# Attention layer for eight batches: in the last batch's steps 3 to 10 the second pair of scores goes ahead of the maxima, the turns of y and h use the job bank, and POOL makes h's output for batch 6

## The reference

```python
xn = layer_norm(x, norm_w, norm_b)
q = (xn @ q_w + q_b).reshape(Bx, Tx, H, -1)
k = (xn @ k_w + k_b).reshape(Bx, Tx, H, -1)
att = jnp.einsum('bnhl,bmhl->bnmh', q, k)
att = att + (1.0 - mask) * -1000000.0
att = jax.nn.softmax(att, axis=2)
v = ((xn @ v_w + v_b) * src_mask[:, :, None]).reshape(Bx, Tx, H, -1)
y = jnp.einsum('bnmh,bmhl->bnhl', att, v).reshape(Bx, Tx, Dx)
e = jax.nn.silu(emb) @ emb_w + emb_b
scale, shift = jnp.split(e[:, None, :], 2, axis=2)
h = layer_norm(y, sb_norm_w, sb_norm_b) * (1.0 + scale) + shift
h = jax.nn.silu(h) @ out_w + out_b
return x + h
```

## Time and profile before

| | |
|---|---|
| median of 3 runs | 521.43 us (519.89 to 522.01) |
| profiled execution | 522.72 us, its span 521.0 us |
| busy in the span | PE 503.0, DVE 408.0, ACT 356.2, POOL 225.3 us |
| clock of PE | full in all but the first slices |
| steps 3 to 10 of batch 7 | 465.42 to 494.47 us of the span |
| steps 11 to 15 of batch 7 | 494.47 to 506.8 us |
| last output products, norms and stores | 506.8 to 521.0 us |

### The profile page before, as it was taken

The page is one execution under the profiler, slowest core; times in us unless marked ns, Lnnn a source line. Parts: engine busy times, 40 slices in busy tenths (PEclk is TensorE's granted clock), DMA queues, the critical chain, the costliest instruction groups (busy, mean ns, idle before and its releaser), DMA issues.

```text
span 521.0 us, 10061 instructions
## 1 busy us (share of the span) xinstructions
PE 503.0 (97%) x2831; PEld 189.4 (36%) x2834; DVE 408.0 (78%) x657; ACT 356.2 (68%) x647; POOL 225.3 (43%) x270
## 2 busy tenths in 40 slices
PE   8898999999999999999999999999999999998787
PEld 3422333343333333333333434343433333332225
DVE  6696778888798978888788878888788877888714
ACT  2305777667876778677877777677777777666783
POOL 4365324436335643536335543545345444334101
PEclk9989999999999999999999999999999999999999
DMA  5335444234434443235434444235433342234002
GB/s 155 111 116 163 124 124 134 79 93 125 129 89 123 132 140 113 79 101 153 127 99 122 108 132 125 79 107 151 134 102 115 104 133 83 82 113 128 0 2 81
DMA packets 54586, 57.42 MB, mean 110 GB/s; under 512 B 12424, under 2 KB 41736, under 8 KB 54560
## 3 DMA queue, kind: packets, MB, share of 16 engines
q1 hardware_dynamic: 51808, 54.74, 36.0%
q10 hardware_dynamic: 2752, 2.37, 1.6%
HBM read 35.82 MB, written 21.00 MB: 109 GB/s over the span
## 4 chain that ended last, share of the span: by engine, by line
PE 85%; DVE 4%; issue 3%; POOL 3%; ACT 3%; DMA 1%; SPq 0%; POOLq 0%; ACTq 0%; DVEq 0%
PE pv_ps L577 24%; PE st_ps L561 22%; PE mx_ps L525 12%; PE job_ps L640 9%; PE job_ps L649 5%; PE job_ps L661 3%; DVE negmax L952 2%; PE mx_ps L686 2%; ACT probs L745 2%; PE mx_ps L538 2%; PE mx_ps L620 1%; PE mx_ps L694 1%; PE pv_ps L461 1%; DMA k_rows<-qk_dram 1%; DVE x_stats L956 0%
## 5 line engine op out<-in xcount | busy, mean ns | idle before, releaser
L952 DVE TENSOR_REDUCE negmax<-mx_ps 128x2 f32<-128x1024 f32 x256 | 304.7, 1219 | 83.2 <-PE mx_ps L525 82.9
L745 ACT ACTIVATE probs<-st_ps 128x512 f32<-128x512 f32 x502 | 272.3, 595 | 116.5 <-PE st_ps L561 115.8
L561 PE MATMUL st_ps<-q_rows,k_rows 115*128 115x512 bf16 x502 | 155.1, 383 | 3.2 <-ACT probs L745 2.8
L577 PE MATMUL pv_ps<-probs,v_rows 128*32 128x512 f32 x1024 | 136.4, 605 | 0.6 <-ACT probs L745 0.6
L1225 POOL TENSOR_TENSOR qk_parts<-qk_rest,qk_parts 128x512 bf16<-128x512 f32 x31 | 36.0, 1161 | 133.0 <-DVE qk_parts L1026 133.0
L525 PE MATMUL mx_ps<-k_rows,q_rows 51*128 51x512 bf16 x512 | 79.4, 383 | 2.1 <-DMA k_rows<-qk_dram 2.1
L561 PEld LDWEIGHTS st_ps<-q_rows,k_rows 115*128 115x128 bf16 x502 | 39.1, 97 | 105.0 <-ACT probs L745 71.7
L1210 POOL TENSOR_TENSOR qk_parts<-qk_full,zero 128x512 bf16<-128x512 f32 x29 | 30.2, 1042 | 77.1 <-ACT qk_full L767 77.1
L640 PE MATMUL job_ps<-x_norm_t,w_qk 128*128 128x512 f32 x116 | 59.5, 593 | 0.0
L525 PEld LDWEIGHTS mx_ps<-k_rows,q_rows 51*128 51x128 bf16 x512 | 15.8, 94 | 111.0 <-DVE negmax L952 53.0
L1216 POOL TENSOR_TENSOR qk_rest<-qk_full,qk_parts 128x512 f32<-128x512 f32 x31 | 35.9, 1158 | 4.3 <-ACT qk_parts L759 2.0
(11 more groups left out here) (126 smaller groups left out, 390.3 us busy)
## 6 DMA issues: line engine op xcount, KB each, us to landing
qk_dram<-qk_parts SPq DMA_DIRECT2D x128, 128.0 KB
q_rows<-qk_dram SPq DMA_DIRECT2D x124, 96.0 KB, 2.6
k_rows<-qk_dram SPq DMA_DIRECT2D x124, 96.0 KB, 2.6
x_in<-in_x SPq DMA_DIRECT2D x16, 256.0 KB, 3.0
x_res<-in_x SPq DMA_DIRECT2D x7, 512.0 KB, 4.4
out<-out_sb SPq DMA_DIRECT2D x14, 256.0 KB, 2.6
k_rows<-mask_dram SPq DMA_DIRECT2D x64, 6.0 KB
w_e<-in_L_cond_emb_w ACTq DMA_DIRECT2D x4, 256.0 KB, 2.9
```

Source lines behind the costliest of these rows:

```text
L561: pe.matmul(st_bank(b, t, h), k_rows[0:ROWS_ALL, g, h, c * P:(c + 1) * P], q_rows[0:ROWS_ALL, g, h, :], start=True, stop=True).then_inc(st ...
L577: mm = pe.matmul(pv_ps[VW * h:VW * (h + 1), :], v_rows[:, c, g * GH + h, :], probs[:, t % P_SLOTS, h, :], start=(c == 0), stop=(c == CH - ...
L745: act.activation(probs[:, t % P_SLOTS, h, :], st_bank(b, t, h), ACT.Exp).then_inc(exp_done, 1)
L952: dve.tensor_reduce(by_pair[:, :, j, c], mx_ps[j][:, :, :], AXIS_X, ALU.max, negate=True).then_inc(max_done, 1)
```

## The change

All of it concerns batch 7. `short(b, t)` holds for its steps from 3 on.

- PE's order in short steps: scores 0 and 1, value product, scores 2 and 3, small turn, quad, side. (In wide steps there are no quads left, and the order stays.)
- In short steps the sides use `job_ps` in place of the first bank of `mx_ps[0]`. They wait for `out_ready` of batch 5 and for the reader of the side before, and no longer for a reduction; the quad no longer waits for the reader of a side. ACT and DVE read the turned tile from there.
- The first of the late output products waits for the read of the third turn of y of batch 7, as both use `job_ps`.
- `h_t` of batch 6 is made by POOL with four `tensor_tensor` (two for each half), in place of two `scalar_tensor_tensor` on DVE. They stand in POOL's program behind the bias on x_res. `h_lin` enters twice: h_tanh * h_lin + h_lin.

```diff
-LAST_LATE = {(2, 1): ("proj", 3, 0), (7, 2): ("hturn", 0, -1), (8, 2): ("hturn", 1, -1)}
+LAST_LATE = {(2, 1): ("proj", 3, 0)}
+SHORT_STEP = 3
+def short(b, t):
+
+    return isinstance(b, int) and b == B - 1 and t >= SHORT_STEP
...
+        def side_bank(b, t):
+
+            return job_ps[:, :] if short(b, t) else mx_ps[0][:, 0, :]
...
-                    if j == 0 and side_at(b, t - 1):
+                    if j == 0 and side_at(b, t - 1) and not short(b, t - 1):
...
                 if i == 0 and 0 in halves:
                     pe.wait_ge(h_ready, KD * (B - 1))
-                    pe.wait_ge(out_ready, 2 * (B - 2))
+                    pe.wait_ge(y_ready, NG * (B - 1) + NG - 1)
...
-                ps = mx_ps[0][:, 0, :]
+                ps = side_bank(b, t)
...
+                if short(b, t):
+                    pe.wait_ge(out_ready, 2 * (B - 2))
...
-                pe.wait_ge(max_done, PAIRS * (STEPS * mb + step) + 1)
+                if not short(b, t):
+                    pe.wait_ge(max_done, PAIRS * (STEPS * mb + step) + 1)
...
-                    max_turn(b, t)
+                    if not short(b, t):
+                        max_turn(b, t)
...
                     pv_step(b, t)
-                    max_quad(b, t)
+                    if not short(b, t):
+                        max_quad(b, t)
                     if not wide(b, t):
                         st_unit(b, t, 2)
                         st_unit(b, t, 3)
+                    if short(b, t):
+                        max_turn(b, t)
+                        max_quad(b, t)
...
-                    act.activation(h_lin[:, i, :], mx_ps[0][:, 0, :], ACT.Identity, bias=mod_now[:, 1, i:i + 1],
+                    act.activation(h_lin[:, i, :], side_bank(b, t), ACT.Identity, bias=mod_now[:, 1, i:i + 1],
...
-                    by_head = mx_ps[0][:, 0, :].rearrange("p (c h w) -> p c h w", h=GH, w=VW)
+                    by_head = side_bank(b if t >= 0 else b - 1, t if t >= 0 else t + STEPS).rearrange("p (c h w) -> p c h w", h=GH, w=VW)
...
+                if isinstance(b, int) and b == B - 1:
+                    for i in range(KD):
+                        pool.wait_ge(h_tanh_ready, KD * (B - 2) + i + 1)
+                        pool.wait_ge(turned["outp"], 2 * (B - 2))
+                        pool.tensor_tensor(h_tanh[:, i, :], h_tanh[:, i, :], h_lin[:, i, :], ALU.mult).then_inc(h_mixed, 1)
+                        pool.wait_ge(h_mixed, i + 1)
+                        pool.tensor_tensor(h_t[:, i, :], h_tanh[:, i, :], h_lin[:, i, :], ALU.add).then_inc(h_ready, 1)
```

More of the change, by code:

```diff
@@ L352, in attention_layer @@
         h_tanh_ready = sem("h_tanh_ready")
+        h_mixed = sem("h_mixed")
         h_ready = sem("h_ready")
```

## The result

The changed kernel takes 518.37 us (median of 14 runs, 517.24 to 520.40) against 521.23 (14 runs, 519.87 to 522.03). The ratio is 0.9949 with a 95% interval of 0.9936 to 0.9962, so 2.7 us faster with an interval of 2.0 to 3.3. The prediction was 518.9. The gain lies at the edge between "faster by over 0.5%" and "within 0.5%", where the forecast had put it.

The account below looks back on a forecast made before the run. No engine was full; DVE was taken to bound steps 3 to 5 of batch 7, PE's written order the rest. Step 12 starting 2.5 us earlier, other terms 0, gave 518.9 us from the median 521.43; range 517.3 to 521.2.

Parts of the forecast that it names:

- The spacings: Times between operations on PE, ACT and DVE, read from the old trace; old order reproduced to about 0.15 us.
- the walk: Steps 3 to 12 of batch 7 worked through in the new order: step 12 starts 2.55 us earlier, say 2.5.
- One sign of being right: Step 12's first score waits on the rows' DMA and starts 2.2 to 2.3 us after the last split.
- The side turns: Turns of h in steps 6 and 7 and of y in step 9: 1.63, 2.03 and 2.72 us earlier.
- rival 3: Side turns still wait for a reduction while quads go later: 2.1 us slower, 523.5; chance 0.05.
- The rows of maxima: Group 3's rows, moved by two DMAs, land 0.35 us after PE is free and hold step 12's first score.
- Rival 1: The maxima's rows don't hold step 12, which starts at 493.5: gain 3.2 us, 518.2; chance 0.16.
- DVE's idle time: DVE waits about 1 us before each quad of steps 7 to 9 in the new order.
- rival 2: DVE starves behind later quads; last split and step 12 gain only 0.5 to 1 us: 520.6; chance 0.24.
- rival 4: The change does nothing, as the last split stays at 493.3: 521.4 us; chance 0.05.
- Steps 3 to 5: no gain for the maxima: DVE bounds these steps, so PE's time won there is not won in the maxima; split about 477.79 for 477.9.
- Their going is worth 0: Taking two 0.68 us instructions for h off DVE, in steps 7 and 8, gains 0; bounds 0 to 0.68.

Follow-up runs that it names:

- b_order_only: Changed kernel with only PE's new order kept: side turns stay in the first maxima bank, h's sums on DVE; stretch 33.27 us against 31.68 before, ratio 1.0021.
- h_rows_late: Changed kernel with one more 4 KB DMA on SP ahead of group 3's two row DMAs; stretch 29.57 us against 29.21.
- e_two_queues: Changed kernel with the second row DMA of group 3 issued by ACT instead of SP; stretch 28.85 us against 29.21, ratio to before 0.9953.
- f_short5: Changed kernel with the new order and bank from step 5 on, not step 3; stretch 29.82 us against 29.21, ratio to before 0.9978.
- d_dve_h: Changed kernel with h of batch 6 kept on DVE's two instructions, not POOL; stretch 29.77 us against 29.21, ratio to before 0.9981.
- j_dve_h_apart: As d_dve_h, but POOL's sum on x_in waits until both DVE instructions for h are through; stretch 29.20 us, ratio to before 0.9950.
- a_bank_only: Changed kernel with only the side turns' bank change kept, PE's order and h's place as before; stretch 30.75 us against 31.68 before, ratio 0.9998.
- k_best: As e_two_queues, with step 6's small turn straight behind the value product; stretch 28.58 us, ratio to before 0.9938.
- l_side_first: As e_two_queues, with the turn of h ahead of the quad in steps 6 and 7; stretch 27.75 us, ratio to before 0.9919.

## Why the prediction was right, point by point

**The spacings.** Set off by the 0.14 by which step 3 starts later in the profile after, the walk against the trace reads: turn of h in step 6 at 478.14 (measured 478.16), h_lin 478.81 (478.86), exponentials of step 7 at 479.49 (479.54), second h_lin 482.19 (482.22), exponential 2 of step 8 at 484.83 (484.84), quad of step 9 at 487.85 (487.86), turn of y 488.39 (488.40), small turn of step 10 at 490.92 (490.86), last split ended 491.82 (491.80), step 12 at 494.15 (494.25). Of these the last alone is over 0.06 off: I had step 12 start with the landing. Of the walk's other times the small turn of step 6 is furthest off, by 0.10 (476.89, measured 476.79). One sign of being right was missed a little: step 12 started 2.45 after the split, for 2.2 to 2.3.

**The side turns** came 1.6 earlier in step 6, 2.0 in step 7 and 2.7 for the turn of y in step 9, as worked out. The run b_order_only shows what rival 3 would have cost: the mechanism was real (1.59), but the bank's change takes it away. Its size was walked too high. The prediction had 2.1 for the order alone, by a last split 3.0 later than before. It came 2.6 later. So the walk's accuracy in the changed kernel does not hold for every order, and no run shows which spacing was off there.

**The rows of maxima** hold step 12 by 0.46 (0.35 forecast). Rival 1 fell by that, and the runs h_rows_late and e_two_queues show the wait from both sides. The measured landing of 1.7 to 1.8 held again. With the 2.0 that the Trainium skill ("DMA: Bandwidth & Descriptors", section "Anatomy of one DMA — SWDGE (gpsimd) path") gives for the other issue path, step 12 would by my estimate have come 0.25 later than it did, so the trace does not bear that figure out for this queue. The forecast's lower edge, a gain of 2.0, took a landing of 2.3, for which the earlier trace rows give no ground.

**DVE's idle time** before the quads of steps 7 to 9 came as walked (1.49, 1.00 and 1.16), and cost no more than that: rival 2 did not happen. Nor did rival 4, since the last split came at 491.94 and not at 493.3.

**"Steps 3 to 5: no gain for the maxima"** was right as arithmetic, since the split of step 6 ends nearly where it did (11.70 for 11.78 after step 3's value product). As a reading it misleads: f_short5 shows that without those steps the split is 0.6 late. What the prediction called no gain is a gain of 0.6 and a loss of 0.6.

**"Their going is worth 0"**, of DVE's two instructions for h, is the step that failed. I had priced 0.68 against DVE's idle time and given bounds of 0 to 0.68 for its own time, but not looked at what POOL does at that moment in the new order. d_dve_h and j_dve_h_apart show 0.56, all of it by the collision with the sum on x_in. That 0.56 lies within the bounds of 0 to 0.68 is luck: they were worked out for another mechanism. It did not harm the total, since the walk of the changed kernel had neither the instruction nor the collision in it. POOL's four sums took 1.27 each for the 1.16 that I took, and ended at 487.32, 18 us ahead of their reader.

**The size.** 2.5 forecast, 2.47 measured in the stretch; 2.7 (2.0 to 3.3) over whole runs. Only the stretch is fine enough to test the walk. Whole runs would bear out anything from 2.0 to 3.3.

## What to carry to other kernels

When each engine's order is written by hand and none is full, walk the new order with spacings read from the old trace, and walk the old order too: where that reproduces the trace, the new walk is worth trusting to a tenth or two of a microsecond. Here it came within 0.15 us for the changed kernel and in a_bank_only, f_short5, e_two_queues, k_best and l_side_first. It was 0.5 off for the order alone, and it knows nothing of two engines that hinder each other (0.56 in d_dve_h). A wait taken away (the bank) and a move (the order) can have opposite signs alone and a gain together, so price them together. An instruction that seems free because its engine idles is free only if nothing that it contends with runs beside it, as POOL's sum did here: check what the shift brings next to it.

## What the runs showed of the hardware

- A DVE scalar_tensor_tensor of 128x512 with both inputs in SBUF took 2.39 us, for 0.68, when it started 0.51 after a POOL tensor_tensor of 2.36 us. The profile shows no idle time there; the instruction itself is long. A POOL copy of 128x4 took 0.68, for 0.19, when it started 0.04 after such a DVE instruction.
- Two 4 KB DMAs of one queue start 0.5 to 0.6 apart, and a DMA to a DRAM tensor ahead of them took 0.39. Issued from SP and ACT, they start 0.18 apart.
- Whole executions scatter before the first value product of batch 0: it starts at 45.08 in the profile before, 45.19 in the one after and at 42.61 in i_again (the same kernel as after, span 516.1 for 518.7). From 20 to 30 us the granted clock was 0.83 in the first two and 1.00 in i_again. The clock is not the whole of it: in a_bank_only it was 1.00 too, and the first value product came at 44.71. The cause stays open. From there on the two profiles of the changed kernel run in step. A difference of 0.1 us in the last batch is therefore readable in single profiles, while single executions scatter by 3 us. The row is of i_again:
```profile
42.61 1.07 PE L589 MATMUL pv_ps<-probs,v_rows 128*32 128x512 f32 x8
```
